# A four-layer graph network on one core: GpSimd's scratch fills taken out, the masks of the first repeated depth moved to PSUM, and one edge tile of the relational pass moved from TensorE's fetch to GpSimd's gather

## The reference, cut to what matters

```
h = relu(layernorm(x)); x = x + L0(h)   # weighted sum of the neighbours' rows
h = relu(layernorm(x)); x = x + L1(h)   # message network, summed at the source
h = relu(layernorm(x)); x = x + L2(h)   # relational: msg = (h[src] @ W_rel[type]) * e
h = relu(layernorm(x)); x = x + L3(h)   # 4 depths: msg = h[src] @ w(edge); w is made once
```

## Time and profile before

| what | value |
|---|---|
| median of 3 runs | 24924.08 us (24918.77 to 24929.06) |
| the profiled execution | 24893.96 us, span 24892.2 us |
| granted TensorE clock, mean over the span | 0.925 |
| busy | TensorE 85%, GpSimd 78%, VectorE 70%, ScalarE 59% |

### The profile page before, as it was taken

How to read it: one execution, slowest core, us unless ns; L and a number is a source line. 1 busy time by engine, 2 the same in 40 slices (tenths; PEclk the granted TensorE clock), 3 DMA queues, 4 the chain that set the end, 5 groups by cost and what they waited for, 6 DMA issues and landing times. The chain is left out here.

```text
span 24892.2 us, 403534 instructions
## 1 busy us (share of the span) xinstructions
PE 21275.5 (85%) x110422; PEld 11977.0 (48%) x110422; DVE 17478.9 (70%) x29340; ACT 14674.0 (59%) x24676; POOL 19392.5 (78%) x21213
## 2 busy tenths in 40 slices
PE   7999578888888999988888888799979999688886
PEld 4555255555555666654444444344434444333333
DVE  6555378888877888875555555688868888566665
ACT  7888411111115777754444444788868888577775
POOL 6777678888886888877777777777777777788887
PEclk9999789999999999998999998899989999898997
DMA  3222145555552222223333333566656666455554
GB/s 101 42 42 42 39 89 95 92 93 94 92 92 69 75 75 75 75 63 106 114 115 113 114 114 112 161 199 199 199 154 200 201 200 200 137 162 164 162 162 125
DMA packets 2192586, 2964.43 MB, mean 119 GB/s; under 512 B 778166, under 2 KB 1678244, under 8 KB 2190948
## 3 DMA queue, kind: packets, MB, share of 16 engines
q1 hardware_dynamic: 1340898, 2776.49, 34.2%
q0 software_dynamic: 782304, 157.92, 9.6%
q10 hardware_dynamic: 69282, 28.92, 0.4%
HBM read 2289.02 MB, written 672.64 MB: 119 GB/s over the span
## 5 line engine op out<-in xcount | busy, mean ns | idle before, releaser
L777 POOL DMA_INDIRECT got<-table,idx x14040 | 13721.3, 977 | 4390.6 <-issue 3967.9
L797 PE MATMUL in_place<-place_hot,tparts 128*128 128x512 fp8e4 x49950 | 11542.9, 390 | 1657.8 <-ACT place_hot L1002 1654.3
L1002 ACT ACTIVATE place_hot<-place_b,far_lanes 128x512 fp8e4<-128x512 f16 x17550 | 10959.5, 704 | 8.5 <-PE in_place L797 8.5
L797 PEld LDWEIGHTS in_place<-place_hot,tparts 128*128 128x128 bf16 x49950 | 4940.3, 101 | 7537.9 <-issue 2331.3
L1606 POOL DMA_INDIRECT added<-rows,add_idx x2160 | 3602.9, 1668 | 717.4 <-issue 659.0
L1178 DVE TENSOR_TENSOR prod<-w_in,rows_p 128x2048 f32<-128x2048 f32 x810 | 1853.1, 2288 | 1638.1 <-ACT rows_p L990 1609.8
L1649 PE MATMUL acc<-hot,spread 128*128 128x392 bf16 x12960 | 2545.2, 350 | 0.0
L1223 DVE TENSOR_TENSOR prod<-wcopy,got 128x1024 f32<-128x1024 f32 x810 | 983.6, 1231 | 1823.1 <-DMA got<-table,idx 1289.5
L1232 DVE TENSOR_REDUCE msg<-prod 128x64 f32<-128x1024 f32 x1620 | 1967.7, 1215 | 41.4
L1191 DVE TENSOR_REDUCE msg<-prod 128x128 f32<-128x2048 f32 x810 | 1853.0, 2288 | 105.4
L866 PE MATMUL wmat<-k,h 128*128 128x256 f32 x6480 | 1785.9, 400 | 0.0
(11 more groups left out here) (250 smaller groups left out, 21552.6 us busy)
## 6 DMA issues: line engine op xcount, KB each, us to landing
w_in<-kept SPq DMA_DIRECT2D x2430, 512.0 KB
kept<-wcopy SPq DMA_DIRECT2D x810, 512.0 KB, 2.7
got<-table,idx POOLq DMA_INDIRECT x14040
attr<-in_edge_attr SPq DMA_DIRECT2D x270, 768.0 KB
place_b<-place_row SPq DMA_DIRECT2D x1350, 128.0 KB
range_b<-range_row SPq DMA_DIRECT2D x1350, 128.0 KB
rows<-in_src_row SPq DMA_DIRECT2D x270, 512.0 KB
sums<-outb SPq DMA_DIRECT2D x1350, 96.0 KB
```

What stands on the lines that cost most here:

```text
L777: pool.indirect_dma_start(out=got[:, r, j * W:(j + 1) * W], out_offset=None, in_=table, in_offset=bass.IndirectOffsetOnAxis(ap=idx[:, r, j ...
L797: mm = pe.matmul(in_place[b][:, h, :], tparts[:, s, t, :], place_hot[:, b, t, h * XC:(h + 1) * XC], start=(t == 0 and s == 0), stop=(t == ...
L1002: ins = act.activation(place_hot[:, b, t, :], place_b[:, b, :], ACT.Abs_reciprocal_sqrt, bias=SB["far_lanes"][:, t:t + 1], scale=HOT_SLOPE ...
```

## The change

Three things are changed in `edge_pass`. The argument `fill` and all that hangs on it go away: the tile `rest`, the fills and the semaphore `rested`. `mask` is in PSUM in every `kernel_kept` pass, which is new for depth 1 alone. `X` of the relational pass is 3 in place of 4: nine tiles are gathered, and three are fetched by TensorE.

```diff
-RW = 256
@@ build
-        edge_pass(nc, a, SB, "weighted", table16, fill=False)
+        edge_pass(nc, a, SB, "weighted", table16)
@@
-            edge_pass(nc, a, SB, "kernel_kept" if depth else "kernel_net", table16, fill=depth == 3, psum_mask=depth >= 2)
+            edge_pass(nc, a, SB, "kernel_kept" if depth else "kernel_net", table16)
@@ edge_pass
-    X = {"weighted": 4, "relational": 4, "kernel_net": 0, "kernel_kept": 4}[kind]
+    X = {"weighted": 4, "relational": 3, "kernel_net": 0, "kernel_kept": 4}[kind]
@@
-        if fill:
-            rest = sb("rest", [P, J0 * RW])
@@
-        if psum_mask:
+        if kind == "kernel_kept":
             mask = [ps(f"mask{k}", [P, 512])[:, 0:F * CW].rearrange("p (f j) -> p f j", f=F) for k in range(HALVES)]
@@ gpsimd, chunk
-                    if fill and at != 0:
-                        pool.wait_ge(S["rested"], k)
                     pool.sem_inc(S["turn_open"], 1)
                     for j in range(J0):
                         pool.indirect_dma_start(
                             out=got[:, r, j * W:(j + 1) * W], out_offset=None, in_=table,
                             in_offset=bass.IndirectOffsetOnAxis(ap=idx[:, r, j:j + 1], axis=0)).then_inc(got_in[r], 16)
-                        if fill:
-                            ins = pool.memset(rest[:, j * RW:(j + 1) * RW], 0.0)
-                    if fill:
-                        ins.then_inc(S["rested"], 1)
```

More of the change, by code:

```diff
@@ L565, in rounds, with edge_pass @@
         body(k, k % RING, k // RING, k)
-def edge_pass(nc, a, SB, kind, table, fill=True, psum_mask=False):
+def edge_pass(nc, a, SB, kind, table):
     W = 32 if kind == "relational" else 16
     F = 32 if kind == "relational" else 16
-    X = {"weighted": 4, "relational": 4, "kernel_net": 0, "kernel_kept": 4}[kind]
+    X = {"weighted": 4, "relational": 3, "kernel_net": 0, "kernel_kept": 4}[kind]
     FW = D + 1 if kind == "relational" else D
@@ L650, in edge_pass @@
                  "attr_used0", "attr_used1", "w_made", "w_used", "h1_made", "h1_ready", "h2_made", "h2_ready",
-                 "hot_made", "hot_used", "out_made", "stored0", "stored1", "dve_step", "run_cleared", "rested", "turn_open", "fetch_open",
+                 "hot_made", "hot_used", "out_made", "stored0", "stored1", "dve_step", "run_cleared", "turn_open", "fetch_open",
                  "place_in0", "place_in1", "range_in0", "range_in1", "places_hot", "in_place_made", "picked_made", "in_row_made", "fetched",
```

## The result

The changed kernel takes 23974.03 us (median of 4 runs, 23937.52 to 23981.22) against 24926.57 us (4 runs, 24918.77 to 24943.07). The ratio is 0.9614, with a 95% interval of 0.9597 to 0.9631. It is 952.5 us faster, where 854 were forecast, and lies in the range given.

The account below looks back on a forecast made before the run. GpSimd was taken to bound depths 2 and 3, GpSimd and TensorE together the relational pass. Gains 608 + 12 + 233 = 853 us off 24894 give 24041, plus 30 to the median 24070 us; range 23950 to 24220.

Parts of the forecast that it names:

- Depth 3: Third depth: GpSimd bound it with the fills on its path; without them it becomes as long as depth 2, gaining 608 us.
- Depth 1: First depth: with the mask in PSUM the scan no longer stalls gathers, gaining 12 us, bounds 0 and 15.
- The relational pass: GpSimd and TensorE each fill the 12.82 us chunk; relieving both gives 11.96 us a chunk, a gain of 233 us.
- so I keep 0.078 for each of nine: 0.70 us: Relational pass: VectorE's instructions keep stalling gathers by 0.078 us each, adding 0.70 us to GpSimd's 11.26 us a chunk.
- GpSimd sets 11.96 us a chunk, VectorE is 0.2 under it: Relational pass after the change: GpSimd's gathers with stalls set 11.96 us a chunk; VectorE needs 11.75, TensorE 1.4 less.
- the rival in which VectorE's rate decides: Relational pass settles without stalls, VectorE sets 11.5 us a chunk: 124 us more gain, 23946 us; chance 0.08.
- VectorE's own term: Relational pass: 12.82 us less 0.93 of waiting for `wmat` and 0.13 from `picked` leaves 11.75 us a chunk.
- TensorE's clock: Relational pass: granted clock, 1.00 before, would go under 1.00 as TensorE's pause becomes 1.4 us a chunk.
- The rival in which it falls: Relational pass: TensorE at 1.2 GHz in stretches, 24215 us (chance 0.13), or throughout, near 26500 us (chance 0.02).
- The sentence in the prediction that every pass with pauses had a clock under 1.00: Kernel before: passes with TensorE pauses ran partly at 1.2 GHz, clock 0.96 in depths 1 and 2, 0.90 elsewhere.
- What the profile should show: Depth 3: 1600 gathers in 2000 us; depth 1: 946 ns gathers; relational: 1.02 us gathers, VectorE waiting 0.2 us for rows.
- The sign that I had named for VectorE as the limit: Relational pass: if GpSimd waits for `idx` in the profile after, VectorE is the limit.

## Why the prediction came out as it did

*Depth 3* was right in mechanism and size: 608 forecast, 613 measured, and 597 for the whole kernel when done alone.

*Depth 1* was right: 12 forecast, 17 measured, and the run with the mask alone shows that the mask does it. Five of the 17 are not the mask's, as depth 2 gave them too.

*The relational pass* was right in direction and in the step that both full engines had to be relieved; the two runs with one edit show it. The term was mis-sized: 233 us forecast, 329 measured, 11.96 us a chunk against 11.60. The step that failed is "so I keep 0.078 for each of nine: 0.70 us". I took the stalls of before for a cost of GpSimd's gathers that comes with VectorE's instructions. The run without fills points to what they were: room that GpSimd had beside TensorE's pace, since that run gained 17 us only, with 419 us of waiting in the window. That they cost nothing before was not tested by itself. Now they are 0.37 us a chunk, as much as nine gathers lack to VectorE's chunk, and they follow VectorE's pace and GpSimd's own work. So "GpSimd sets 11.96 us a chunk, VectorE is 0.2 under it" had the order wrong, and the rival in which VectorE's rate decides (chance 0.08, 11.5 us) was the nearest, though that rival had the stalls gone. That the time still lies in the range is in part luck: the range's low end, 24 us under the measured time, had been set by that rival.

*VectorE's own term* was 11.75 us and measured 11.60. `picked` takes 0.133 us less to the next start, as taken, and the wait for `wmat` gave 0.90 of the 0.93. What the sum left out is that two other instructions became shorter: from the start of `onehot` to the next start 0.616 us before and 0.535 after, from the copy of the carry to the last reduction 0.414 and 0.317. Before, 8500 to 10500 us:

```profile
L1087 DVE TENSOR_SCALAR onehot<-types,iota_col 90x1536 bf16<-90x1536 f16 x156 | 108.1, 693 | 28.0 <-DVE msg L1232 17.7
...
L1128 DVE COPY msg<-run 128x32 f32<-128x32 f32 x156 | 45.5, 292 | 5.4
```

After, and then the run with X = 3 and fills, in the same window:

```profile
L1078 DVE TENSOR_SCALAR onehot<-types,iota_col 90x1536 bf16<-90x1536 f16 x172 | 106.0, 616 | 30.9 <-PE wmat L863 9.8 <-DVE msg L1223 9.8
...
L1119 DVE COPY msg<-run 128x32 f32<-128x32 f32 x172 | 33.6, 196 | 5.9
```

```profile
L1087 DVE TENSOR_SCALAR onehot<-types,iota_col 90x1536 bf16<-90x1536 f16 x144 | 97.5, 677 | 25.8 <-DVE msg L1232 15.9 <-PE wmat L872 0.5
...
L1128 DVE COPY msg<-run 128x32 f32<-128x32 f32 x143 | 42.7, 299 | 4.9
```

In the relational pass this last run differs from the changed kernel by the fills alone, and its two instructions are as long as before; without fills and with X = 4 they take 620 and 223 ns. So GpSimd's work in the kernel before also made VectorE slower, and the prediction had only the other direction, VectorE stalling GpSimd.

*TensorE's clock* was forecast under 1.00 and stayed at 1.00, 2.4 GHz, although TensorE now pauses. The rival in which it falls didn't come, and VectorE waits 10 us of 2000 for `wmat`. By the rule of the Trainium skill that pauses between groups of matmuls can make the clock swing ("TensorE: Matmul & The Clock Gate", HAM oscillation) it could have fallen; the trace didn't show it here. It did fall where the gathers set the pace, 0.94 in the run with X = 3 and fills. The sentence in the prediction that every pass with pauses had a clock under 1.00 did not fit the trace of before either. In the weighted pass TensorE was busy 942 us of 1000 and the clock was 1.00:

```profile
1000.00:2000.00 1000.00, 942.22 (x5656) 505.45 (x5654) 586.82 (x2970) 856.52 (x1490) 758.14 (x794) 1.00 0.22 42
```

*What the profile should show* was right for depths 1 and 3, and wrong for the relational pass: no wait for gathered rows, a mean gather of 986 ns where 1.02 us was named, and TensorE's pause before a group of `wmat` (155.9 us in the window), not before `in_row`. The sign that I had named for VectorE as the limit, GpSimd waiting for `idx`, did not come, though VectorE was the limit. A limit can hold another engine back without any wait on a semaphore.

The rest that I can't place, some 10 us between the passes and in the first pass, is of the size by which these differ from one execution to the next. The 5 us by which depths 1 to 3 each end earlier than depth 2 did before lie in every gather: the mean is 946.8 ns in depth 2 before and 944.2 after, and 2160 x 0.0026 = 5.6 us. Both lengths occur with the same code of that pass on one chip (946.6 ns in the run with the added reduction, 944.5 in the one with the small fill), so the change doesn't make it. What does stays open.

## What to carry to other kernels

If two engines both fill a period, price the change for both before the gain is booked; either edit alone gave next to nothing or a loss here. A stretched instruction on an engine that is never seen waiting isn't a cost by itself: look whether the stretch just makes up the difference to a slower engine, and test it with a little more work on the one and then on the other. Where the gathers do set the pace, keep one of two inputs of the long VectorE instructions in PSUM where a trace shows gathers starting under them, and count an instruction by the time to the next start, not by its length.

## What the runs showed of the hardware

- A gather that starts under a scan with both inputs in SBUF lasts until the scan's end and about 0.75 us on: scan from 9009.03 to 10.05, gather from 9009.53 to 10.81, in the rows of one chunk above. In the changed relational pass 262 of the 266 gathers that started under the scan were stretched, by its rest less 0.19 us; the other four started within 0.04 us of the scan's start.
- Where the inputs lie decides: under the product with both in SBUF (first depth of the changed kernel) all 341 gathers that started with over 0.25 us of it left were stretched, and none of 468 under the product with `wmat` in PSUM (its relational pass).
- Two SBUF inputs are not the only case. `onehot` reads one tile and a column. In the run with the fill of 256 columns 235 gathers started under it with over 0.25 us of it left, and all were stretched. Under the reductions of the changed relational pass none of 277 was, and under `picked` none of 264 in the run with that fill.
- It works in both directions: with the fills `onehot` and the copy of the carry took 677 and 299 ns, without them 616 and 196, X being 3 in both.
- GpSimd can be held to VectorE's pace with no wait on a semaphore in the trace: undisturbed gathers, fill and stalls fill the period in four runs (11.24 + 0.37 = 11.61; 11.24 + 0.19 + 0.19 = 11.62; 11.24 + 0.32 = 11.56; 11.24 + 0.16 = 11.40).
- A fill of 64 columns between two gathers cost 0.024 us of GpSimd's time, one of 256 columns 0.186: the pause of 0.305 us between gathers covers the short one.
- Two stretches with nearly the same busy time of TensorE, 1844 and 1849 us of 2000, had granted clocks of 1.00 and 0.96 (relational pass and depth 1 of the changed kernel).
